# One kernel, two feed-forward starts: block 0's first feed-forward goes alone over both partition halves, block 1's moves into the first iteration

## The reference, cut to what matters

```
ln(x)  = (x - mean) / sqrt(var + 1e-5)
ffn(x) : s = x @ Win + bin            # 512 -> 64
         h = relu(s[..., None] * W1 + b1)      # 64 x 16
         g = sum(h * W2, -1) + b2              # 64
         return g @ Wout + bout                # 64 -> 512
attn(x): q, k, v = split(x @ w_attn); q, k = elu(q) + 1, elu(k) + 1   # 16 heads of 32
         causal linear attention: y = (q . S) / (q . z + 1e-6), S = running sum k v, z = running sum k
         return y @ w_proj
x = x + 0.5 * ffn(ln(x))
x = x + attn(ln(x))
x = x + 0.5 * ffn(ln(x))
```

## Time and profile before

| what | value |
|---|---|
| median of 3 runs | 2358.32 us (2357.66 to 2359.26) |
| the profiled execution: its own time | 2360.11 us |
| its span, first to last instruction | 2358.3 us |
| mean granted TensorE clock | 0.985 |
| busy: TensorE, VectorE, ScalarE, GpSimd | 2272.6, 1932.4, 1425.8, 810.8 us |

### The profile page before, as it was taken

How to read it: one execution, slowest core, us unless ns; L and a number is a source line. 1 busy time by engine, 2 the same in 40 slices (tenths; PEclk the granted TensorE clock), 3 DMA queues, 4 the chain that set the end, 5 groups by cost and what they waited for, 6 DMA issues and landing times.

```text
span 2358.3 us, 74773 instructions
## 1 busy us (share of the span) xinstructions
PE 2272.6 (96%) x32578; PEld 1767.1 (75%) x32578; DVE 1932.4 (82%) x3346; ACT 1425.8 (60%) x2267; POOL 810.8 (34%) x864
## 2 busy tenths in 40 slices
PE   3999999999999999999999999999999999999995
PEld 2777777777777777777777777777777777777774
DVE  6679888888888889888889888879888889887766
ACT  5556657556556556657566657556657566657554
POOL 5233233333233333233333233333233333233222
PEclk7999999999999999999999999999999999999997
DMA  5001101111111111112111101111111111101111
GB/s 175 20 20 38 53 24 57 56 56 37 40 37 56 56 56 38 51 25 56 56 56 38 56 21 56 55 56 37 53 23 56 56 56 38 56 21 39 38 38 37
DMA packets 49656, 111.52 MB, mean 47 GB/s; under 512 B 8241, under 2 KB 10289, under 8 KB 45234
## 3 DMA queue, kind: packets, MB, share of 16 engines
q1 hardware_dynamic: 49330, 106.74, 15.3%
HBM read 72.12 MB, written 34.60 MB: 45 GB/s over the span
## 4 chain that ended last, share of the span: by engine, by line
PE 94%; DVE 2%; issue 1%; SPq 1%; ACT 0%; DMA 0%; POOL 0%; DVEq 0%; ACTq 0%; POOLq 0%
PE bank L1011 39%; PE att L1011 24%; PE att L1127 6%; PE att L1152 6%; PE att L1040 6%; PE att L1069 3%; PE bank L1078 2%; PE att L1143 2%; PE bank L1115 2%; PE bank L1163 1%; PE bank L1069 1%; DVE acc_psum L717 1%; PE att L1095 1%; PE bank L1095 1%; DMA qT<-in_L_attn_w_attn_dram 0%
## 5 line engine op out<-in xcount | busy, mean ns | idle before, releaser
L458 ACT ACTIVATE xhat<-res,nmr,rstd 128x512 f32<-128x512 f32 x384 | 302.6, 809 | 361.8 <-DVE nmr L687 290.6
L475 ACT ACTIVATE ffr<-ffs,b1c,w1c 128x512 f32<-128x512 f32 (+2 forms) x544 | 424.4, 805 | 19.6 <-DVE acc_psum L717 13.3
L717 DVE SCALAR_TENSOR_TENSOR acc_psum<-ffr,w2c,acc_psum 128x512 f32<-128x512 f32 (+2 forms) x510 | 378.8, 743 | 48.6 <-ACT ffr L475 27.3
L371 POOL TENSOR_SCALAR_AFFINE_SELECT A<-A 128x512 f32<-128x512 f32 x256 | 156.6, 635 | 711.2 <-ACT A L435 711.2
L360 POOL TENSOR_TENSOR res<-res,hbout 128x512 f32<-128x512 f32 x256 | 351.8, 1391 | 4.0 <-ACT xhat L458 3.4
L679 DVE BATCH_NORM_STATS2 st<-res 128x6 f32<-128x512 f32 x384 | 260.6, 679 | 16.4 <-DMA res<-in_L_attn_x_dram 10.8
L367 POOL TENSOR_TENSOR A<-qT,A 128x512 f32<-128x512 f32 x128 | 165.2, 1294 | 240.2 <-DVE zc L762 116.4
L1011 PE MATMUL att<-xh,wa_h 128*128 128x512 f32 x584 | 233.4, 400 | 1.9 <-DVE xl L696 1.9
L1011 PE MATMUL att<-xl,wa_h 128*128 128x512 f32 x584 | 231.3, 396 | 0.0
L1011 PE MATMUL att<-xh,wa_l 128*128 128x512 f32 x584 | 231.2, 396 | 0.0
L338 POOL TENSOR_SCALAR nmr<-mv 128x4 f32<-128x4 f32 x96 | 21.9, 228 | 555.4 <-DVE mv L681 555.4
(11 more groups left out here) (142 smaller groups left out, 5149.1 us busy)
## 6 DMA issues: line engine op xcount, KB each, us to landing
xf<-scratch SPq DMA_DIRECT2D x128, 256.0 KB, 4.5
res<-in_L_attn_x_dram SPq DMA_DIRECT2D x31, 1024.0 KB, 5.3
out_dram<-res SPq DMA_DIRECT2D x31, 1024.0 KB, 5.7
scratch<-rden SPq DMA_DIRECT2D x128, 8.0 KB, 1.7
res<-in_L_attn_x_dram SPq DMA_DIRECT2D x4, 256.0 KB, 3.1
kT<-in_L_attn_w_attn_dram SPq DMA_DIRECT2D x1, 1024.0 KB, 5.5
qT<-in_L_attn_w_attn_dram SPq DMA_DIRECT2D x1, 1024.0 KB, 11.0
v<-in_L_attn_w_attn_dram SPq DMA_DIRECT2D x1, 1024.0 KB, 14.3
```

What stands on the lines that cost most here:

```text
L371: eng.affine_select(out=A[:, h, :, :], in_=A[:, h, :, :], compare_op=ALU.is_ge, fill=0.0, base=0, pattern=[[0, 4], [1, P]], channel_multip ...
L458: eng.activation(xhat[t % 2][:, :], res[b % SLOTS][:, t, :], ACT.Identity, bias=nmr[:, n, b % 2, t:t + 1], scale=rstd[:, n, b % 2, t:t + 1 ...
L475: eng.activation(ffr[i % 2][p, w], ffs[p, w], ACT.Relu, bias=b1c[p, i:i + 1], scale=w1c[p, i:i + 1]).then_inc(s_hr, 1)
L717: eng.scalar_tensor_tensor(psum[p, w], r[p, w], w2c[p, i:i + 1], psum[p, w], ALU.mult, ALU.add).then_inc(s_hm, 1)
```

## The change

- Block 0's first feed-forward becomes index j = -2 and is laid over both partition halves (`alone`, `only`, `halves`, `columns`), as the last one was: 256 columns in place of 512 for each of its steps. `ff_in` and `ff_out` take the two such cases in one branch.
- Block 1's first feed-forward (j = -1), over both halves too, goes into iteration 0: its `ff_in` between the projections, its sixteen steps between the projections' copies, its `ff_out`, additions and statistics ahead of the first scores.
- SP issues Wout and k's weights ahead of the small weights, and block 1's load behind them. Block 0's shift on VectorE no longer stands behind block 1's statistics.
- GpSimd's low parts of the weights are spread between the layer norms; the copies of ScalarE too.
- In `give`, den, v and k's group 3 are dealt from RING, k's groups 0 and 2, q's last groups and key from ATT, and in TensorE's order scores(j, 1) goes ahead of channels(j + 1, 0).
- Small moves in the order of VectorE, ScalarE and GpSimd in every iteration: ynorm(j, 0) ahead of hidden(j, 5), the masks one step apart, L1 normalisations between the first projections' copies, the first L2 normalisation later, and others.

```diff
+        def alone(j):
+            return j < 0 or j == NB
+        def only(j):
+            return (0, NB - 1) if j == NB else (1, j + 2)
...
-        give_all("in", -1, 0)
-        for b in range(2):
-            give(ATT + RING, ("o1", b, 0), ("o1", b, 1), ("o1", b, 2), ("o1", b, 3))
+        give_all("in", -2, 0)
+        give(ATT + RING, ("o1", 0, 0), ("o1", 0, 2), ("o1", 0, 1), ("o1", 0, 3))
...
-            give(ATT + RING, ("k", j, 0), ("k", j, 1), ("q", j, 0), ("q", j, 1), ("k", j, 2), ("k", j, 3), ("q", j, 2), ("q", j, 3), ("v", j, 0), ("key", j, 0), ("den", j, 0))
+            give(ATT, ("k", j, 0))
+            give(ATT + RING, ("k", j, 1), ("q", j, 0))
+            if j == 0:
+                give_all("in", -1, 0)
+            give(ATT + RING, ("q", j, 1))
+            give(ATT, ("k", j, 2))
+            give(RING, ("k", j, 3))
+            give(ATT, ("q", j, 2), ("q", j, 3))
+            give(RING, ("v", j, 0))
+            give(ATT, ("key", j, 0))
+            give(RING, ("den", j, 0))
...
# SP
-            load(1)
             eng.dma_start(bout_st[0:1, :], ...)
             (win, four transfers)
+            (wo_st, two transfers)
+            eng.dma_start(wa_st[1][:, :, :], wa_v[:, :, C:2 * C]).then_inc(s_wa[1], 16)
             (w1c, b1c, w2c, binc, b2c, ten transfers)
-            eng.dma_start(wa_st[1][:, :, :], wa_v[:, :, C:2 * C]).then_inc(s_wa[1], 16)
+            load(1)
+            (wa_st[0], wa_st[2])
             load(2)
...
# VectorE, head
             for t in range(TILES):
                 stats(L1, 0, t)
-            stats(L1, 1, 0)
-            stats(L1, 1, 1)
             shift(L1, 0)
...
+            for t in range(TILES):
+                stats(L1, 1, t)
+            for i in range(INNER):
+                hidden(-2, i)
+            sums(-2)
...
# VectorE, iteration 0, ahead of the masks of scores(0, 0)
+                if j == 0:
+                    ff_out(1, 1, 0)
                 hidden(j, 0)
+                if j == 0:
+                    ff_out(1, 1, 1)
+                    ff_out(1, 1, 2)
+                    ff_out(1, 1, 3)
+                    stats_of_sum(L2, 1, 0)
+                hidden(j, 1)
+                if j == 0:
+                    stats_of_sum(L2, 1, 1)
                 mask(j, 0, 1)
+                if j == 0:
+                    stats_of_sum(L2, 1, 2)
+                    stats_of_sum(L2, 1, 3)
+                hidden(j, 2)
                 mask(j, 0, 3)
...
# TensorE
                     project(j, 1, 0)
                     project(j, 1, 1)
                     project(j, 0, 0)
+                if j == 0:
+                    ff_in(-1, 0)
                     project(j, 0, 1)
+                if j == 0:
+                    ff_in(-1, 1)
...
                     ff_in(j, 1)
+                if j == 0:
+                    ff_out(-1, 0)
+                    ff_out(-1, 1)
...
                     values(j, 3, 1)
+                    scores(j, 1)
                 if on(j + 1):
                     channels(j + 1, 0)
                 if on(j):
-                    scores(j, 1)
                     outer(j, 0, 0)
```

More of the change, by code:

```diff
@@ L412, in _ @@
                     mask(j, 1, 2)
+                if on(j - 1):
+                    bias(0, j - 1, 1)
+                if on(j):
                     mask(j, 2, 0)
                     mask(j, 2, 2)
+                    mask(j, 3, 0)
+                    mask(j, 3, 2)
                 if on(j - 1):
@@ L1012, in split3, with ff_in @@
                 return op
-            def ff_in(j, part, slots=(0, 1)):
-                if part == 0 and 0 in slots:
+            def ff_in(j, part):
+                if part == 0:
                     take_all("in", j, 0)
                 e.wait_ge(s_win, 64)
-                if j == NB:
-                    e.wait_ge(s_tr[0], 4 * NB)
-                    for c in range(C // D // PARTS * part, C // D // PARTS * (part + 1)):
+                n_c = C // D // PARTS
+                chunks = range(n_c * part, n_c * part + n_c)
+                if alone(j):
+                    half, b = only(j)
+                    e.wait_ge(s_tr[half], 4 * b + TILES)
+                    for c in chunks:
                         for n in range(2):
@@ new lines, in ff_in, with ff_out @@
+                if part == PARTS - 1:
+                    op.then_inc(s_fi, 1)
+            def ff_out(j, t):
+                if alone(j) and t >= 2:
+                    return
+                e.wait_ge(s_ul, j + 3)
+                e.wait_ge(s_wol, 1)
+                if alone(j):
+                    half, b = only(j)
+                    outs = [(n, half, b, t + 2 * n) for n in range(2)]
+                else:
+                    outs = [(n, n, b, t) for n, b in ((0, j - 1), (1, j + 2)) if on(b)]
+                o = [take(f"o{half}", b, i) for n, half, b, i in outs]
@@ L1179, in _ @@
             eng.matmul(o[:, :], tri[0:1, :], bout_st[0:1, :], start=True, stop=True).then_inc(s_mbout, 1)
-            for n in range(2):
-                for part in range(PARTS):
-                    ff_in(-1, part, (n,))
-            for b in range(2):
-                for t in range(TILES):
-                    ff_out(-1, t, (b,))
+            for part in range(PARTS):
+                ff_in(-2, part)
+            for t in range(2):
+                ff_out(-2, t)
             for t in range(TILES):
```

357 lines of the change are left out of this document (209 added, 148 removed).

## The result

| | before | after |
|---|---|---|
| median of the runs, us | 2358.62 (2357.66 to 2359.26, 4 runs) | **2346.26** (2342.73 to 2347.02, 4 runs) |
| ratio, 95% interval | | 0.9942 [0.9929, 0.9954] |
| span of the profiled execution, us | 2358.3 | 2345.3 |

The change makes the kernel 0.6% faster, by 12.4 us; 2344 was predicted, in a range of 2335 to 2355. The total came out, but two of its terms did not, and they were wrong in opposite directions.

A forecast was written before the change was run, and what follows sets the result against it. TensorE, busy for 96% of the span, was taken to bound the kernel. The terms -12.4 + 9.8 - 7.1 - 4.5 = -14.2 us, from the median 2358.32, gave 2344 us, range 2335 to 2355.

The forecast's parts named there:

- A, the head: Stretch up to the first projection: that projection comes at 52.0 us instead of 64.39, a gain of 12.4 us.
- B, iteration 0: Iteration 0 takes on block 1's feed-forward: 5.6 us of work and 4.3 of waits, +9.8 us in all.
- 0.7, 1.4 and 2.1: TensorE's waits in iteration 0, in us: for ff_in's bias copy, before scores(0,0) for the additions, before attend(0,0) for the masks.
- a floor in cycles: Iteration 0's ff_in: a per-matmul floor of some 60 cycles would give 2.2 us in place of 4.2.
- C, den's bank: Odd iterations: den gets a bank of the ring, so TensorE's 16 waits for den's reader go, -7.1 us.
- D, the order moves: Steady iterations: attend's second half follows its first 0.14 us sooner, 32 times, -4.5 us.
- the lost cover: Steady iterations: scores(j,1) ahead of channels(j+1,0) has less cover for its low part, a loss of at most 0.1 us.
- The tail keeps its form: End of the kernel, after the loop: form unchanged, no gain or loss counted.
- the first, that iteration 0 eats the head's gain: Rival: VectorE late for every mask, or block 1's load late; head and iteration 0 near 0, 2350 us, chance 0.15.
- Rivals 3 and 4: scores(j,1) waits for yl each iteration, 2357 us, chance 0.10; the split comes after the normalisation, 2371 us, chance 0.08.
- rival 2: Order moves take more: odd iterations fall to the even ones' pace, tile 2's wait goes too; 2336 us, chance 0.15.
- the signs named in advance: First projection at 51 to 54 us, no wait for den's reader, odd iterations 69.9 to 70.1, even 70.2 to 70.4.

The follow-up runs named there:

- a_guard: The changed kernel with GpSimd again waiting for block 0's second layer norm shift before its low parts of the weights: 2342.19 us, repeated at 2341.27.
- b_noguard: The kernel before without GpSimd's wait for the shift of block 0's second layer norm: 2362.5 us, ratio 1.0012.
- a_halves: The changed kernel with GpSimd's low part of q's weights made by two instructions of 256 columns instead of one of 512: 2344.07 us.
- a_lofirst: The changed kernel with GpSimd's low part of q's weights ahead of rstd of block 0's second layer norm, no wait added: 2345.31 us.
- b_dsecond: b_scores plus the new order of VectorE and ScalarE from tile 0's masks on, and GpSimd's whole new order: 2348.48 us.
- b_moves: The kernel before with all the loop's new banks and order moves, but the old head and no block 1 in iteration 0: 2347.09 us.
- b_scores: b_den with scores(j,1) ahead of channels(j+1,0) on TensorE and no other engine's order touched: 2348.25 us.
- b_den: The kernel before with only den's bank dealt from the ring of three: 2351.78 us, ratio 0.9968.
- a_order: a_guard with the odd masks of scores(0,0) ahead of block 1's statistics on VectorE in iteration 0: 2347.46 us.

## Why the prediction was right, and where it was not

**A, the head: right up to 44 us, then 4.3 us short.** The step that failed is the sentence on the weights, "GpSimd some 4 us later would hold VectorE, and TensorE only after the banks run out". It asks only who waits for GpSimd's results. In the sum it is the term from ff_out to the first projection, 16.5 + 0.3, which measured 21.1 (56.33 - 35.21). What the removed wait had kept apart were two instructions that share no data. a_guard, b_noguard, a_halves and a_lofirst show that the shift is held by whichever long GpSimd instruction has begun just before it, some 0.06 us here, until that one ends. The Trainium skill has this rule (SBUF — State Buffer, SBUF: two separate sides): VectorE and GpSimd share a pair of ports, and if a VectorE instruction with two inputs in SBUF meets a GpSimd one that reads SBUF, whichever starts first holds the pair for its whole length and the other is blocked. The trace agrees: the shift reads mv and rstd and is held for 4.45 us, while the statistics that start at 49.79, with one input, take 0.66 beside a GpSimd instruction of 4.52 that began at 49.00. That the ports are what ties the two is the page's explanation; the runs show the hold and what ends it. By that rule the sum would have been 4.3 us higher, 2348, and I hadn't weighed it. The trace of before had the hold already, at this very kind of instruction, here in iteration 2 beside `bias`, and in the mean of its group:
```profile
211.73 1.29 POOL L360 TENSOR_TENSOR res<-res,hbout 128x512 f32<-128x512 f32 x1
```
```profile
212.24 0.80 DVE L687 SCALAR_TENSOR_TENSOR nmr<-mv,rstd 128x4 f32<-128x4 f32 x1
```
```profile
L687 DVE SCALAR_TENSOR_TENSOR nmr<-mv,rstd 128x4 f32<-128x4 f32 x96 | 33.7, 351 | 45.9 <-POOL rstd L340 45.9
```
Both rows end at 213.0. In before one shift is held so in each of 28 iterations, and one in the head (1.23 us at 29.26); the earlier trace rows has only the 0.15 of one that was not. In b_dsecond, b_moves and the changed kernel, where the bias stands elsewhere, those of the loop are gone, which has brought TensorE nothing: b_scores still has them, and its odd iterations take the same 69.72.

**B, iteration 0: +9.8 predicted, +9.9 and +10.5 in the two profiles of the changed kernel.** The waits were found and priced well: 0.7, 1.4 and 2.1 against 0.6, 1.2 and 2.5. The third was a slip of addition: 3.4, twice 0.75 and twice 0.68 are 6.3 and not 6.1, and 6.3 less 3.9 is 2.4. Missed was scores(0,1), 0.7. ff_in(-1) was too dear: 3.2 us (twice 1.59), against 4.2 from the tail's row. ff_out took 1.8 (95.03 to 96.80) against 1.4. So the sum is 3.2 + 1.8 + 5.0 = 10.0, and the longer start at half the clock adds 0.65 in the first profile. The rule of the Trainium skill that was weighed there (TensorEngine Tiling (Array Packing), Instruction Overhead), a floor in cycles, gave 2.2 us: the trace agrees neither with that halving nor with the recorded 4.2, since a record takes 12.4 ns here (1.59 over 128) at a granted clock of 1.00, and 17.6 in the tail at 0.50 (4.5 over 256), faster, but not twice as fast.

**C, den's bank: -7.1 predicted, all of it there.** The waits are gone, and b_den shows the term alone: 8.0 us in the runs, with an interval of 4.5 to 10.6.

**D, the order moves: -4.5 predicted.** The step was mis-sized, and in part wrong about which move does it. Between the profiles of b_den and the changed kernel iterations 1 to 29 lose 7.3 us (2039.84 - 2032.57), where 29 times 0.14 is 4.1. The prediction counted attend's second half (0.14, measured 0.17), and neither the update's start (0.08) nor the stretch ahead of attend (0.14). It gave the 0.14 to GpSimd's earlier masks, but b_scores, where GpSimd's order is that of before, has the 0.43 too; that the scores themselves are made earlier before attend, and with them all masks, is the likelier reason, and is argued only. It set ynorm's move, which it took to be what keeps the low part in time, against the lost cover; b_scores leaves ynorm where it was and has no more waits. What ynorm's move gains there is lost in an even iteration at tile 0: the update of tile 0 comes 39.25 us after the iteration's start in the changed kernel, 39.08 in b_scores and before.

**The tail: nothing predicted, some 2 us lost.** "The tail keeps its form" holds for the work, but its ff_in has 3.1 us of issue gaps where it had 0.9:
```profile
2320.99 2.25 PE L1148 MATMUL att<-xf,win 32*64 32x64 f32 x128 [1.84 <-issue]
2324.46 0.50 PE L1148 MATMUL att<-xf,win 32*64 32x64 f32 x9 [1.22 <-issue]
```
It is not the spread of single profiles: the gaps sum to 2.8 to 3.4 us in all seven profiles of the changed kernel and its variants and in b_moves, and to 0.9 to 1.3 in before, b_noguard, b_den, b_scores and b_dsecond. b_dsecond and b_moves differ by the banks and the order of the projections' half, so the loss comes with these; what makes the gaps stays open.

**The rivals.** Of the first, that iteration 0 eats the head's gain, one half is what happened: by all profiles together A + B is near 0. But D was not halved, and its reason, VectorE late for every mask, was no more than what B had counted; the missing gain was lost in the head. With the wait put back, head and iteration 0 do win: iteration 1 starts at 133.63 and 135.44 in the two profiles of a_guard, and a_guard is 4.9 us under b_moves on the same chip. Rivals 3 and 4 did not occur. Of rival 2 a part did, in the odd iterations: 69.73, below the 69.9 that I had given them.

That the total came within 2.3 us of the forecast is in part luck. The head gave 4.3 us less than it could and the tail lost some 2 that nobody had counted; against them the loop gave 1 to 2 more than forecast, and the profile of before, from which the terms were read, had the earliest of five heads and 3.1 us of single gaps in its loop. The changed kernel was 12.4 us under before in the first runs and 15.7 in the second. Of the signs named in advance two failed: the first projection at 51 to 54 (56.33 and 55.45), and odd iterations at 69.9 to 70.1 (69.73).

## What to carry to other kernels

A wait between two engines that share no data may be there to keep their instructions apart: before it is taken out, look at what would start beside what, and above all whether a long GpSimd instruction begins just before a short VectorE one with two inputs in SBUF, like this shift, on the critical path. The hold does not show as idle time but in the length of the held instruction, so look for one whose mean is far above its shortest. Cutting the long one in pieces bounds the hold by one piece, and a wait of 0.3 us removes it. When an instruction is put later on one engine, follow the queue of every engine that waits for it, as in a_order, where statistics and a shift moved on VectorE held ScalarE for 6 us.

## What the runs showed of the hardware

- A VectorE instruction of 128 x 4 elements took 4.45 us beside a GpSimd instruction of 4.49 (after), and 2.30 beside one of 2.34 (a_halves); where GpSimd waited for it, it took 0.16 (a_guard). Beside a GpSimd instruction of 1.29 that had begun 0.5 us earlier it took 0.80 (before).
- A record of ff_in with 64 columns took 12.4 ns at a granted clock of 1.00 (after, iteration 0) and 17.6 at 0.50 (before, tail).
- Issue gaps of 0.3 to 0.8 us came in b_scores before the same matmul in ten iterations, and at that matmul in none of the changed kernel's. In the tail's ff_in such gaps sum to 2.8 to 3.4 us in eight profiles and to 0.9 to 1.3 in five. The profile names nothing that TensorE waited for, and what makes them was not tried.
